# Loading layer 1's constants from SyncE's queue, behind the shared weights, in place of GpSimd's queue

## The reference

```python
# layer 0: a mixture of experts with a shared expert
def _gemma_mlp(x, g, u, d):                    # 256 -> 1024 -> 256
    return (gelu(x @ g) * (x @ u)) @ d
w, sel = top_k(softmax(cond_8), 2)             # 2 of 8 experts for each batch
x = x + sum_e dense_w[:, e] * _gemma_mlp(x, skill_gate[e], skill_up[e], skill_down[e]) \
      + _gemma_mlp(x, shared_gate, shared_up, shared_down)

# layer 1: a linear layer plus eight LoRA adapters of rank 16, weighted by cond_8
out  = einsum('btc,oc->bto', x, W_base) + b_base
h    = einsum('btc,erc->bter', x, As)
lora = einsum('bter,eor,be->bto', h, Bs, cond_8)
x = x + out + lora * 2.0
```

## Time and profile before

| | |
|---|---|
| median of the runs | 849.15 us |
| profiled execution | 848.08 us |
| its span, first to last instruction | 846.3 us |
| TensorE busy | 826.7 us, 98% |
| VectorE, ScalarE, GpSimd busy | 464.4, 360.5, 9.2 us |
| granted TensorE clock, mean | 0.998 |
| moved by DMA | 62.95 MB, 74 GB/s over the span |

### The profile page before, as it was taken

One profiled execution on the slowest core, in us unless ns is written; L12 is line 12 of the kernel. 1 busy time (PEld: TensorE's weight loads), 2 busy tenths in 40 slices (PEclk: granted clock), 3 DMA queues, 4 the chain that ended last, 5 costly groups with the idle time before them and its releaser, 6 DMA issues.

```text
span 846.3 us, 10976 instructions
## 1 busy us (share of the span) xinstructions
PE 826.7 (98%) x3766; PEld 687.9 (81%) x3766; DVE 464.4 (55%) x682; ACT 360.5 (43%) x583; POOL 9.2 (1%) x20
## 2 busy tenths in 40 slices
PE   4899999999999999999999999999999999999997
PEld 3688888888888888888888888888888888888886
DVE  3665645555555555546465554564645646455553
ACT  3554434444343534344344444343534444334442
POOL 4000000000000000000000000000000000000000
PEclk9999999999999999999999999999999999999999
DMA  4742301313032230322303131132211313014000
GB/s 126 247 131 70 109 29 58 117 58 118 0 99 75 74 99 0 99 74 74 99 12 125 37 112 62 37 99 66 82 62 37 120 54 94 18 39 136 1 1 25
DMA packets 59651, 62.95 MB, mean 74 GB/s; under 512 B 4144, under 2 KB 56368, under 8 KB 59632
## 3 DMA queue, kind: packets, MB, share of 16 engines
q1 hardware_dynamic: 58944, 61.88, 23.4%
q0 software_dynamic: 544, 0.79, 0.4%
q10 hardware_dynamic: 144, 0.03, 0.0%
HBM read 58.49 MB, written 4.19 MB: 74 GB/s over the span
## 4 chain that ended last, share of the span: by engine, by line
PE 96%; DMA 2%; DVE 0%; SPq 0%; ACT 0%; issue 0%; DVEq 0%
PE ps_acc L262 31%; PE ps_gate L262 31%; PE ps_up L262 31%; PE ps_misc L262 3%; DMA raw_dn<-_L_cond_shared_down_dram 2%; PE ps_misc L299 1%; DVE x_lo L483 0%; SPq L182 0%; SPq L181 0%; DVE x L564 0%; DVE sh_gu_lo L483 0%; DVE o_row L580 0%; ACT x_hi L395 0%; ACT sh_gu_hi L395 0%; PE ps_misc L329 0%
## 5 line engine op out<-in xcount | busy, mean ns | idle before, releaser
L395 ACT CAST inner_hi<-inner 128x512 fp32r<-128x512 f32 x192 | 119.2, 621 | 316.9 <-DVE inner L600 201.0
L483 DVE TENSOR_TENSOR inner_lo<-inner,inner_hi 128x512 fp32r<-128x512 f32 x192 | 133.0, 693 | 129.3 <-ACT inner_hi L395 129.3
L600 DVE SCALAR_TENSOR_TENSOR inner<-gelu,coef_now,ps_up 128x512 f32<-128x512 f32 x128 | 95.6, 747 | 133.5 <-PE ps_up L262 133.5
L432 ACT ACTIVATE gelu<-ps_gate 128x512 f32<-128x512 f32 x192 | 114.1, 594 | 116.2 <-PE ps_gate L262 115.6
L483 DVE TENSOR_TENSOR ex_gu_lo<-raw_gu,ex_gu_hi 128x1024 fp32r<-128x1024 f32 x64 | 78.5, 1226 | 51.4 <-ACT ex_dn_hi L395 51.4
L262 PE MATMUL ps_gate<-x_cur_hi,ex_gu_hi 128*128 128x512 f32 x256 | 100.5, 392 | 0.0
L262 PE MATMUL ps_gate<-x_cur_lo,ex_gu_hi 128*128 128x512 f32 x256 | 99.8, 390 | 0.0
L262 PE MATMUL ps_acc<-inner_hi,ex_dn_lo 128*128 128x512 f32 x256 | 99.8, 390 | 0.0
L262 PE MATMUL ps_acc<-inner_hi,ex_dn_hi 128*128 128x512 f32 x256 | 99.8, 390 | 0.0
L262 PE MATMUL ps_gate<-x_cur_hi,ex_gu_lo 128*128 128x512 f32 x256 | 99.8, 390 | 0.0
L262 PE MATMUL ps_up<-x_cur_hi,ex_gu_hi 128*128 128x512 f32 x256 | 99.7, 390 | 0.0
(11 more groups left out here) (95 smaller groups left out, 1173.0 us busy)
## 6 DMA issues: line engine op xcount, KB each, us to landing
raw_gu<-n_L_cond_skill_gate_dram SPq DMA_DIRECT2D x64, 256.0 KB, 2.9
raw_gu<-in_L_cond_skill_up_dram SPq DMA_DIRECT2D x64, 256.0 KB, 3.3
raw_dn<-n_L_cond_skill_down_dram SPq DMA_DIRECT2D x64, 256.0 KB, 3.7
x_nat<-in_x_dram SPq DMA_DIRECT2D x8, 512.0 KB, 4.8
out_dram<-o_row SPq DMA_DIRECT2D x16, 256.0 KB, 4.0
raw_gu<-_L_cond_shared_gate_dram SPq DMA_DIRECT2D x4, 256.0 KB, 4.3
raw_gu<-in_L_cond_shared_up_dram SPq DMA_DIRECT2D x4, 256.0 KB, 4.8
raw_dn<-_L_cond_shared_down_dram SPq DMA_DIRECT2D x4, 256.0 KB, 5.9
```

The costliest lines, as they stand in the source:

```text
L395: return nc.scalar.copy(dst, src)
L432: nc.scalar.activation(gelu[:, k % 2, :], ps_gate[k % 2][:], ACT.Gelu_apprx_tanh).then_inc(gelu_done, 1)
L483: return V.tensor_tensor(dst, src, hi.bitcast(F32), ALU.subtract)
L600: V.scalar_tensor_tensor(out=inner[:, k % 2, :], in0=gelu[:, k % 2, :], scalar=coef_now[:, s:s + 1], in1=ps_up[k % 2][:], op0=ALU.mult, op ...
```

## The change

The fourteen DMAs of layer 1's constants are taken out of GpSimd's program and put into SyncE's, behind the shared weights and ahead of the routed ones. Sources, destinations and semaphores stay. GpSimd now ends with the identity matrix. On TensorE, VectorE and ScalarE no instruction moves.

```diff
@@ -220,6 +220,21 @@
                     sp.wait_ge(raw_landed[j - 1], 48)
                 load_pair(j, sg, su, sd)
 
+
+            sp.dma_start(a_nat[:], lora_a.rearrange("e r c -> (e r) c")).then_inc(layer1_landed, 16)
+            for c in range(HC):
+                sp.dma_start(b_nat[:, c, :].rearrange("p (e r) -> p e r", e=E),
+                               lora_b[:, c * P:(c + 1) * P, :].rearrange("e p r -> p e r"))\
+                    .then_inc(layer1_landed, 16)
+            sp.dma_start(w_nat[:], w_base.rearrange("(c p) h -> p c h", p=P)).then_inc(layer1_landed, 16)
+            for i in range(2):
+                sp.dma_start(bias[:, i, :], b_base.partition_broadcast(P)).then_inc(layer1_landed, 16)
+
+            with nc.allow_non_contiguous_dma(reason="64 scalars, each to 16 partitions"):
+                for e in range(E):
+                    sp.dma_start(lora_w[e * R:(e + 1) * R, :],
+                                   cond[:, e].partition_broadcast(R)).then_inc(lora_w_landed, 16)
+
             sp.wait_ge(experts_known, 1)
             load_routed(0, 0, range(PAIRS))
             batch_row(0, True, False)
@@ -237,21 +252,6 @@
...
-            pool.dma_start(a_nat[:], lora_a.rearrange("e r c -> (e r) c")).then_inc(layer1_landed, 16)
...
-                    pool.dma_start(lora_w[e * R:(e + 1) * R, :],
-                                   cond[:, e].partition_broadcast(R)).then_inc(lora_w_landed, 16)
```

## The result

| | before | after |
|---|---|---|
| median of the runs | 849.64 us | 854.61 us (853.24 to 855.65) |
| ratio | 1 | 1.0058 (95% interval 1.0043 to 1.0073) |
| profiled execution, its span | 848.08, 846.3 us | 855.46, 853.6 us |
| mean granted clock | 0.998 | 0.992 |

The median of before is now over five runs (it was 849.15 us over the first three). The change makes the kernel 5.0 us slower; 853.0 us was forecast, 3.8 us above the 849.15 us of that time.

What follows compares the result with a forecast made beforehand. TensorE bounds the kernel, busy 826.7 of 846.3 us. The 7.3 us saved at the start are swallowed by the wait for R: 848.1 + 3.8 = 851.9 us, 853.0 us with the median's 1.07 us; range 844 to 857 us.

Steps and rivals of the forecast that it cites:

- The removal: At the start: earlier pair 0, no wait for pair 1, no half clock there; TensorE could reach step 5 7.3 us earlier.
- pair 1's stall: SyncE's shared pair 1 stood behind GpSimd's `lora_w` DMAs; without that wait step 2 starts 4.3 us earlier.
- The place of the new wait: ScalarE waits for the first routed pair, so TensorE's step 5 waits for step 3's gelu; its up starts 3.8 us later.
- R: Landing of the first routed pair, behind the moved constants on SyncE's queue: 39.2 us, 3.2 us later than before.
- The issuing: SyncE's fourteen added DMAs take 6.3 us to issue, done with the expert's number by 26.2 us, hidden ahead of 35.4 us.
- The cover of TensorE's turn of the constants: TensorE turns the constants at 26.9 us at the earliest, and they land at about 25.8 us.
- Half clock: TensorE's six gate matmuls behind a wait take 2.93 us in place of 1.36 us: 1.6 us lost.
- The price of `lora_w`: Eight `lora_w` DMAs on SyncE's queue at 1.2 us each, 9.6 us, landing at 35.4 us.
- the elements and not the queue: The 1.2 us go with 4-byte elements, since B's 64-byte pieces went through GpSimd's queue without such a cost.
- the rival on a rhythm: Cheap elements: the 1.2 us belong to GpSimd's queue; up of step 5 4.8 us earlier, 844.3 us; chance 0.20.
- the sign: Whole kernel: the change makes it slower, given 0.65; wrong if `lora_w` lands less than 0.7 us apart.
- The rule on transfers below 512 bytes: Below 512 bytes the DMA engine does a read-modify-write, so `lora_w`'s cost would go along to SyncE's queue.

Runs made afterwards that it cites:

- pool_src_apart: Kernel before, its eight `lora_w` DMAs still on GpSimd's queue but reading 4-byte elements from 128 places (rows of W): 841.56 us, one run.
- the halves: The change in two parts: only the six large constants on SyncE (six_on_sp, 851.14 us), or only the eight `lora_w` DMAs there (lora_on_sp, 851.84 us).
- b_rows: Kernel after, with each of B's two DMAs reading 128 runs of 512 bytes in place of 1024 runs of 64 bytes: 854.88 us, one run.
- bias_apart: onchip_sp, with the two bias DMAs reading 128 different rows of W in place of one shared row: 842.10 us, one run.
- onchip_sp: Kernel after without `lora_w` DMAs: VectorE makes `lora_w` from the logits, the six large constants stay on SyncE: 845.22 us, ratio 0.9947 to before.
- six_on_sp: Kernel after, with the eight `lora_w` DMAs on GpSimd's queue as its first; A, B, W and bias on SyncE: 851.14 us, ratio 1.0022 to before.
- lora_on_sp: Kernel before, with only the eight `lora_w` DMAs moved to SyncE behind shared pair 3: 851.84 us, ratio 1.0027 to before.
- src_apart: Kernel after, with the eight `lora_w` DMAs reading 4-byte elements from 128 places (rows of W) in place of 8 shared ones: 851.68 us, one run.
- dst_apart: Kernel after, with the `lora_w` elements written 256 bytes apart in each partition in place of side by side: 854.61 us, one run.
- run32: Kernel after, with each `lora_w` DMA reading one 32-byte run for each of 16 partitions, 16 pieces in place of 128: 845.54 us, one run.

## Why the prediction was right, and where not

- The removal. Pair 0 was to land at 8.2 us and landed at 8.05 us; pair 2 at 17.5 us, landed at 17.32 us; TensorE's start 10.3 us, was 10.09 us; and no wait for pair 1. Right, and pool_src_apart shows that `lora_w` was the cause of pair 1's stall. Step 2 came earlier than forecast: 4.3 us before 24.39 us, and 1.4 us from the start, make 18.7 us, and it was 17.57 us. The forecast took ScalarE's 18.02 us from the earlier trace rows; but before, the first twelve projection matmuls of TensorE started 0.43 us apart, and after only the first eight, the rest 0.23 us apart. When TensorE came to turn the constants, 8.2 us were in hand (26.03 against 34.21 us), not 7.3 us. The waits behind took all of it.
- The place of the new wait was right: the first routed pair, ScalarE's split, the gelu of step 3. R was put at 39.2 us and came at 40.2 us. That it came so near is in part luck, since two terms were wrong in opposite directions. The constants were to land at 25.8 us and landed at 28.0 us, `lora_w` at 35.4 us and landed at 37.9 us, and R was to follow in 3.8 us and followed in 2.3 us. The six constants were put at 3.8 us for one pair's bytes; the halves show 5.7 to 5.8 us between pair 2 and R, of which b_rows takes away 1.0 us (small pieces) and bias_apart 1.4 us (shared row). `lora_w` was put at 9.6 us and cost 8.7 to 8.9 us between pair 2 and R: 1.3 us for each, not 1.2 us, less what the shorter last part gives back.
- The issuing was to be hidden, with the routed pair issued at 26.2 us. It was issued at 28.58 us, since W's instruction alone took 2.41 us. It was hidden all the same.
- The cover of TensorE's turn of the constants was missing: TensorE was there at 26.03 us, and waited 2.0 us, until 28.07 us. It cost nothing, since R ended later still. In onchip_sp and six_on_sp, where R comes earlier or the constants later, this wait (3.5 and 4.7 us) is the one that counts.
- Half clock: put at 1.6 us. The gate matmuls of step 5 took 2.90 us as taken from the earlier trace rows, but up at 2.56 us was slow too, 1.2 us more, for which the sum had no term. In the profiled execution R's 1.0 us bring the forecast 3.8 us to 4.8 us, and 4.9 us were measured at up of step 5; with the 1.2 us and the 1.5 us of the end, and 0.2 us given back, that is the 7.4 us. The 5.0 us between the medians are not broken down by this: before's median is 1.6 us above its profiled execution, the median after 0.9 us below its own.
- The price of `lora_w` rested on the right row with a wrong reason. I leaned on "the elements and not the queue", and against the rival on a rhythm that was worked out from two landings only. It is not the queue: lora_on_sp has 8.9 us on SyncE's queue. On GpSimd's queue it isn't the 4-byte elements either: from places apart they are cheap. On SyncE's queue about half of it (4.6 of 8.8 us) stays with single elements from places apart, through their issuing. Whether the sign would have held without the slow reads is open: src_apart took 851.68 us in its one run, 0.9 us above the slowest of before's executions, with R at 36.0 us, half clock for twelve matmuls behind the wait (2.90 and 2.56 us), and 4.65 us at the end.
- The rule on transfers below 512 bytes (the Trainium skill, "DMA: Bandwidth & Descriptors", Specifications) decided nothing here: src_apart's elements are as short, and the slowest DMA landed in 3.9 us in place of 10.8 us.

## What to carry to other kernels

Before a DMA is moved to another queue, look for what it holds up, not for what it is queued on: here one whose source was slow to read held up about as much behind either issuer (8.8 us over seven DMAs before, 9.1 us after), and the question was who stood behind it. See whether the value is on chip already: here every partition had it, three VectorE instructions of 0.7 us replaced 9 us of stalled transfers and gave 0.8%, where moving the transfers lost 0.6%. And when a load that leads at the start is sped up, work out anew each landing that TensorE may wait for next, here the routed pair and the constants themselves, with everything that has been put ahead of it. A wait of ScalarE's, however long, counts only if TensorE then waits too (5.2 us in onchip_sp, and none behind it on TensorE).

## What the runs showed of the hardware that I had not expected

- 128 reads of the same eight places, each read by 16 partitions, take 1.25 to 1.3 us on either queue, and the DMA engines are nearly idle meanwhile (shares of 0.02 and 0.05). On SyncE's queue 833 packets passed in 7 us, 8.4 ns each (after); on GpSimd's 158 in 6 us, 38 ns each, for the same pace of whole DMAs. The same number of 4-byte reads from 128 places landed in 2.1 to 3.9 us (src_apart). Whether it is the very same 4 bytes that count or their nearness (eight places within 256 bytes) isn't told apart by these runs; the destination is excluded (dst_apart).
- A transfer stands behind such reads on another queue too: in six_on_sp pair 0, issued by 2.6 us, landed at 12.2 us, with lora_w on GpSimd's queue; without anything on that queue it landed at 8.05 us (after). Why SyncE's packets don't pass those of GpSimd's queue, no run shows.
- With B in 2048 pieces of 64 bytes the next issue on SyncE's queue took 2.41 us, with pieces of 512 bytes 0.44 us.
- How long TensorE's half clock lasted behind a wait did not go by the wait's length. The groups of six matmuls that take 1.36 us at the full clock took 2.93 and 1.43 us behind 4.5 us (before), 2.90 and 2.56 us behind 9.3 us (after) and behind 5.3 us (src_apart), but 2.90 and 1.56 us behind 6.8 us (lora_on_sp), and 2.90 and 1.52 us behind only 2.6 us (run32). The granted clock was 0.50 or 0.51 in each of the first groups.
